# Attention state in 64-token chunks, with TensorE's slot in a new order

## The reference

```python
mod = (_silu(L0_c) @ L0_wmod).reshape(4, 6, 1, -1)     # sa, ca, ga, sb, cb, gb per sequence
h = _layernorm(x) * (1 + ca) + sa
x = x + ga * _L0_attn_ref(h, w_qkv, w_out)
h = _layernorm(x) * (1 + cb) + sb
x = x + gb * _L0_ffn_ref(h, w_router, w_gate, w_down)

# attention, per head; q, k = elu(.) + 1
def step(carry, inp):
    S, z = carry
    q_t, k_t, v_t = inp
    S = S + k_t[..., :, None] * v_t[..., None, :]
    z = z + k_t
    num = einsum('bhde,bhd->bhe', S, q_t)
    den = maximum(sum(z * q_t, -1, keepdims=True), 1e-6)
    return (S, z), num / den
```

## Time and profile before

| | us |
|---|---|
| three runs | 862.91, 864.46, 868.90 |
| median | 864.46 |
| profiled execution, span from first to last instruction | 864.3 |
| PE, PEld busy | 812.9, 667.7 |
| DVE, ACT, POOL busy | 577.1, 488.9, 478.9 |

### The profile page before, as it was taken

One profiled execution on the slowest core, in us unless ns is written; L12 is line 12 of the kernel. 1 busy time (PEld: TensorE's weight loads), 2 busy tenths in 40 slices (PEclk: granted clock), 3 DMA queues, 4 the chain that ended last, 5 costly groups with the idle time before them and its releaser, 6 DMA issues.

```text
span 864.3 us, 24637 instructions
## 1 busy us (share of the span) xinstructions
PE 812.9 (94%) x9527; PEld 667.7 (77%) x9527; DVE 577.1 (67%) x1740; ACT 488.9 (57%) x1003; POOL 478.9 (55%) x621
## 2 busy tenths in 40 slices
PE   6899999999999999999999999868999998999994
PEld 4677776777767767777777677558999998999994
DVE  5676676777777867868767767750756655767762
ACT  4665666656757656657657565442655453555551
POOL 2203345664664665646656646564556657666654
PEclk9999999999999999999999999988999999999997
DMA  5589903333332233322222212334476666676653
GB/s 195 186 247 282 284 26 114 85 87 110 67 120 89 76 114 87 86 101 70 72 71 62 64 50 41 62 85 148 82 158 120 151 145 122 152 152 158 121 100 37
DMA packets 71426, 99.02 MB, mean 115 GB/s; under 512 B 7810, under 2 KB 52866, under 8 KB 71320
## 3 DMA queue, kind: packets, MB, share of 16 engines
q1 hardware_dynamic: 38744, 53.93, 23.0%
q0 software_dynamic: 21760, 31.66, 16.2%
q10 hardware_dynamic: 10816, 11.96, 4.5%
HBM read 46.84 MB, written 63.36 MB: 127 GB/s over the span
## 4 chain that ended last, share of the span: by engine, by line
PE 75%; POOL 6%; DMA 6%; DVE 4%; issue 4%; ACT 3%; POOLq 0%; another core or an unknown queue 0%; SPq 0%; DVEq 0%; ACTq 0%
PE PJ L1436 10%; PE SCW L1662 9%; PE MD L1409 7%; PE SCW L1340 7%; PE SCW L1376 7%; PE PJ L1446 5%; PE SCW L1677 4%; PE SCW L1360 4%; PE SCW L1401 4%; DMA out<-EX,desti 3%; PE MD L1350 3%; PE SCW L1366 2%; PE SB L1677 2%; PE MD L1677 2%; POOL hT L544 2%
## 5 line engine op out<-in xcount | busy, mean ns | idle before, releaser
L494 POOL DMA_INDIRECT slot_rows<-Hrow,sloti x128 | 128.0, 1000 | 129.6 <-PE SCW L1366 48.5
L967 DVE TENSOR_TENSOR Sm<-SCW,tri 128x1024 f32<-128x1024 f32 x128 | 150.7, 1219 | 70.9 <-PE SCW L1340 69.0
L612 POOL DMA_INDIRECT out<-EX,desti x80 | 125.3, 1566 | 24.1 <-POOL idle L440 11.4
L1436 PE MATMUL PJ<-hT,w_qkv 128*128 128x512 f32 x384 | 110.1, 419 | 2.4 <-POOL hT L544 1.9
L440 POOL TENSOR_TENSOR idle<-mhalf 128x1 f32<-128x1 f32 x136 | 58.9, 433 | 78.5 <-DVE EX L1270 47.2
L1436 PEld LDWEIGHTS PJ<-hT,w_qkv 128*128 128x128 f32 x384 | 69.7, 190 | 25.1 <-issue 6.5
L1376 PE MATMUL SCW<-Sm,VA 128*17 128x128 f32 x2048 | 80.8, 275 | 0.2 <-issue 0.2
L1409 PE MATMUL MD<-w_og,ATs 128*128 128x256 f32 x256 | 73.2, 404 | 4.7 <-ACT ATs L824 2.8
L676 ACT ACTIVATE EX<-PJ 128x512 f32<-128x512 f32 x64 | 37.9, 592 | 67.5 <-PE PJ L1436 67.5
L1340 PE MATMUL SCW<-QM,KT 32*128 32x256 f32 x1024 | 73.3, 400 | 0.6 <-ACT OTs L839 0.5
L680 ACT ACTIVATE N<-X,nb,rs 128x256 f32<-128x256 f32 x128 | 66.4, 591 | 12.3 <-POOL nb L554 12.2
(11 more groups left out here) (215 smaller groups left out, 1825.4 us busy)
## 6 DMA issues: line engine op xcount, KB each, us to landing
Hrow<-slot_rows SPq DMA_DIRECT2D x32, 516.0 KB
slot_rows<-erow ACTq DMA_DIRECT2D x1, 10400.0 KB, 46.7
X<-x SPq DMA_DIRECT2D x16, 512.0 KB, 4.8
out<-X SPq DMA_DIRECT2D x16, 512.0 KB
Hrow<-mod_rows SPq DMA_DIRECT2D x16, 512.0 KB
QT<-slot_rows SPq DMA_DIRECT2D x8, 516.0 KB
slot_rows<-Hrow,sloti POOLq DMA_INDIRECT x128
N<-wd SPq DMA_DIRECT2D x4, 512.0 KB
```

Of the source, the lines that this page charges most:

```text
L494: pool.indirect_dma_start(xe, bass.IndirectOffsetOnAxis(sloti[:, par, k, t:t + 1], 0), Hrow[:, par, t, :], None, bounds_check=last_slot, o ...
L612: pool.indirect_dma_start(out, bass.IndirectOffsetOnAxis(desti[s % 2][:, a:a + 1], 0), Ys[s % 2][:, a, :], None, bounds_check=TOK - 1, oob ...
L967: dve.tensor_tensor(o.rearrange("p c (k w) -> p c k w", k=2), SCW[:, 2 * pair:2 * pair + 2, :].rearrange("p k (c w) -> p c k w", c=DC), tr ...
L1436: last = mm(PJ[m % 2][:], w_qkv[:, wp, cc, m * P:(m + 1) * P], hT[:, hp, cc, :], start=(cc + i == 0), stop=(cc == DC - 1 and i == len(SPLI ...
```

## The change

A tile's attention is cut in two chunks k of 64 tokens (`CH = P // 2`), and the state is kept for each chunk (`Sbd` with four places in turn, `state_at`). Only the two 64 x 64 blocks on the diagonal of a tile's scores are computed.

- `scores`: 16 matmuls with 32 rows x 64 weights and 128 moving columns, chunk k into partitions 64k to 64k + 63 of the same bank. SCW's four banks each use 256 of 512 columns.
- `masked_scores`: two instructions of 512 elements, each over two banks; the mask is `tri64`, a 64 x 64 triangle for either half of the partitions.
- `from_state`: per chunk 8 matmuls of 64 columns from that chunk's state; the chunk k waits for `sm_done` 2T + k + 1. `from_tile`: 32 matmuls of 64 rows x 17 weights and 64 columns, unsplit.
- `add_to_state` is done for tile n + 1 in slot n: 16 matmuls of 64 rows, fresh sums of each chunk in the new pair of banks PM, which are also PJ[1] and MD. `state` on VectorE reads them masked as `Snew` and adds twice on SBUF. At the end of a sequence the next state is set to 0. SB now takes the output product and the position sums.
- `columns_and_keys` joins the transposes of An of tile n - 1 and of the keys of tile n + 1, and ScalarE copies them by one instruction (`AK`, 512 columns).
- PE's slot: scores, (at q = 3 later) columns and keys, first stage-1 part, sums from the state, update and sums from the tile, norm transposes, product of n - 1, head rows of n, second stage-1 part. ScalarE's, VectorE's and GpSimd's orders and waits follow; the second norm is done at q = 1 in place of 2, and normalising the heads of tile n is in slot n.

The diff, cut to its core:

```diff
-        Sbd = sb("Sbd", [P, DC, 2, VW])
+        Sbd = sb("Sbd", [P, 4, DC, 2, VW])
+        Snew = sb("Snew", [P, 2, DC * 2, SW])
...
+        PM = ctx.enter_context(nc.psum_tensor("PM", [P, 2, 512], F32))
+        PJ, MD = [PJ0[:], PM[:, 0, :]], PM[:, 1, :]
...
+        OB = SCW[:, :, 0:DC * CH].rearrange("p (k b) (c i) -> p k b c i", k=2, c=DC)
...
+            def masked_scores(T):
+                dve.wait_ge(sc_full, T + 1)
+                at_least(dve, av_done, T - 1)
...
+                for b in range(2):
+                    dve.tensor_tensor(Smh(T % 2)[:, 2 * b:2 * b + 2],
+                                      SCW[:, 2 * b:2 * b + 2, 0:2 * P].rearrange("p r (m i) -> p r m i", i=CH),
+                                      tri64[:].unsqueeze(1).unsqueeze(1).to_broadcast([P, 2, 4, CH]),
+                                      ALU.mult).then_inc(sm_done, 1)
...
+            def state(n, first, second):
+                t = n + 1
+                dve.wait_ge(state_full, t + 1)
...
+                dve.tensor_tensor(Snew[:], PM[:, :, 0:DC * 2 * SW].rearrange("p k (h w) -> p k h w", h=DC * 2),
+                                  headmask[:].unsqueeze(1).to_broadcast([P, 2, DC * 2, SW]), ALU.mult
+                                  ).then_inc(state_read, 1)
+                first()
+                dve.wait_ge(state_read, t + 1)
+                dve.tensor_tensor(state_at(2 * t + 1), state_at(2 * t), Snew[:, 0], ALU.add).then_inc(sbd_half, 1)
+                second()
+                dve.wait_ge(sbd_half, t + 1)
...
+                    dve.tensor_tensor(state_at(2 * t + 2), state_at(2 * t + 1), Snew[:, 1], ALU.add).then_inc(sbd_done, 1)
...
+            def scores(T):
...
+                for cc in range(DC):
+                    for k in range(2):
+                        for r in range(4):
+                            rows = slice(32 * r, 32 * r + 32)
+                            last = mm(SCW[part(k), r, cc * P:(cc + 1) * P],
+                                      KT[rows, gp, cc, q * P + CH * k:q * P + CH * k + CH],
+                                      QM[rows, T % 2, :, cc, part(k)], start=True, stop=True, skip_group_check=True)
+                last.then_inc(sc_full, 1)
...
+            def columns_and_keys(n):
...
+                    for cc in range(DC):
+                        last = pe.transpose(MD[:, cc * P:(cc + 1) * P], a[:, cc * P:(cc + 1) * P], ident[:])
+                if tile_ok(n + 1):
+                    t = n + 1
+                    pe.wait_ge(phi_done, 4 * (t // 4) + 4)
+                    at_least(pe, ak_done, n + 1)
...
+            def from_state(T):
...
+                for k in range(2):
+                    pe.wait_ge(sm_done, 2 * T + k + 1)
+                    for cc in range(DC):
+                        for r in range(4):
...
+                            mm(OB[half, k, r // 2, cc, :],
+                               Sbd[rows, (2 * T + k) % 4, cc, :, :].rearrange("p s w -> p (s w)"),
+                               QT[rows, gp, cc, q * P + CH * k:q * P + CH * k + CH], start=(cc == 0), stop=False,
+                               skip_group_check=True)
...
+            def add_to_state(n, g, routed, step):
+                t = n + 1
...
+                    if routed and step == "columns":
+                        pe.wait_ge(h2t_done, 2 * g + 2)
...
             def logits(g, gn, stage1):
+                pe.wait_ge(state_read, min(4 * gn + 2, TILES))
                 if stage1:
                     pe.wait_ge(h_raw, 2 * (gn + 1) + 2)
...
                 if stage1 and q == 0:
-                    stage1_hi(G, 0)
-                    stage1_hi(G, 1)
-                if group_ok(gn - 1) and q == (2 if gn < GROUPS - 1 else 1):
-                    ln2_norm(it, G, gn, gp)
+                    for cidx in range(DC):
+                        stage1_transposed(G, cidx)
+                        stage1_hi(G, cidx)
+                if tile_ok(n) and tile_ok(n + 1) and q != 0:
+                    next_tile_queries(n)
+                if group_ok(gn - 1) and q == 1:
+                    ln2_norm(G, gn)
```

More of the change, by code:

```diff
@@ L28 @@
 VW = 32
+CH = P // 2
 SW = DH + 1
@@ L311, in group_ok, with head, part @@
             return 0 <= n < GROUPS
-        def halves(it, back):
-            return (it - back) // 2 if isinstance(it, int) else (it - back) // 2
-        def headslot(r):
-            return [2 * r, 2 * r + 1]
+        def head(cc, r, s):
+            return cc * HC + 2 * r + s
+        def part(k):
+            return slice(CH * k, CH * k + CH)
         @block.sync
@@ L791, in slot_ @@
                     act.activation(lgT[:], PJ[1][:, 0:P], ACT.Copy).then_inc(lgt_done, 1)
-                if tile_ok(n + 1) and q != 3:
-                    next_tile_queries(T, q, gp, tp, n)
-                if routed and step in ("first", "pick"):
-                    take(lg, lg_ps[:, :, 0:E], lg_full, g)
+                if n >= -1 and q != 3:
+                    columns_and_keys(n)
                 if routed and step == "columns":
@@ new lines, in from_tile @@
+            def from_tile(T):
+                q, gp = T % 4, (T // 4) % 2
+                if q % 2 == 0:
+                    pe.wait_ge(pj_read, 6 * (T // 4) + 5 + q // 2)
+                for cc in range(DC):
+                    for b in range(2):
+                        for k in range(2):
+                            for a in range(4):
+                                r, s = 2 * b + a // 2, a % 2
+                                last = mm(OB[32 * a:32 * a + SW, k, b, cc, :], VA[part(k), gp, q, head(cc, r, s), :],
+                                          Smh(T % 2)[part(k), r, 2 * cc + s, :], start=False, stop=True,
+                                          skip_group_check=True)
+                last.then_inc(av_done, 1)
@@ L1351, in head_rows @@
                 last.then_inc(on_full, 1)
-            def from_state(T, q, gp):
-                at_least(pe, sbd_done, T)
-                pe.wait_ge(sm_done, 2 * T + 1)
-                for cc in range(DC):
-                    for r in range(4):
-                        rows, half = slice(32 * r, 32 * r + 32), slice(64 * (r % 2), 64 * (r % 2) + 64)
-                        mm(OB[half, r // 2, cc, :], Sbd[rows, cc, :, :].rearrange("p s w -> p (s w)"),
-                           QT[rows, gp, cc, q * P:(q + 1) * P], start=(cc == 0), stop=False, skip_group_check=True)
@@ L1574, in slot_ @@
                 if tile_ok(n) and n > 0:
-                    scores(T, q, gp, tp)
-                if routed and step in ("first", "pick"):
-                    logit_rows(g)
+                    scores(n)
+                if n >= -1 and q != 3:
+                    columns_and_keys(n)
                 if n == TILES - 3:
```

449 lines of the change are left out of this document (210 added, 239 removed).

## The result

The kernel before took 865.2 us and the changed one 927.7 us on the same chip (medians of four runs each): ratio 1.073, 95% interval 1.069 to 1.077. Slower by 62 us, where 23 us less was forecast.

The account below looks back on a forecast made before the run. TensorE's instructions were taken to bound attention. Block savings of 39 us, 3 from the dropped state reload and 5 from VectorE, less 24 of added waits, made 23 us off 864.3: 841 us, range 806 to 872.

Parts of the forecast that it names:

- The step that failed: Attention's 64 tiles: TensorE is busy 518 of 535 us, so its instructions' time, block after block, sets a tile's cost.
- Rival (C): Narrow records of scores, state, tile and update supplied too slowly: break-even 14.2 ns each, 897 us at 17.5; chance 0.10.
- the block of L1391 at 285.18: State block of the kernel before, running at 14.4 ns a record behind a gap; taken as the slow bound on pace.
- PE does not wait for its rows; 0: GpSimd and SP in attention: moving row sends to other signals was priced at 0.
- wrong outright: Stated failure signs: the expert stage moves, or PE's clock falls below 1.00 in attention because of new gaps.
- Block terms: Per tile on PE: scores save 0.47 us, sums from the state cost 0.02, sums from the tile save 0.22, update costs 0.23.
- (D): Rival: only four strips run side by side though eight are addressed, in scores and sums from the tile: 875 us; chance 0.07.
- An's and the keys' transposes: On PE, joined into one block of four: 0.57 us instead of 0.37 + 0.37, saving 0.17 a tile.
- Keys behind phi: At q = 3, PE's key transposes of the next tile wait for VectorE's phi: stall 0.5 us per group, 15 groups.
- Router behind h_raw: At q = 0, PE's router matmuls wait for both of ScalarE's h_raw copies: stall 0.6 us per group, 15 groups.
- Update behind h2T: At q = 0, the state update waits until ScalarE has copied both h2T halves: stall 0.5 us per group, 15 groups.
- GpSimd is busy 287 of 535 us: Ground for pricing the moved row sends at 0; if cover failed, each held-up send costs at most 1.0 us per group.

Follow-up runs that it names:

- a_quiet: Changed kernel, gate rows loaded only for the first two groups, four of each group's 512 output rows stored: ratio 1.013 (866.8 us), second run 1.030 (889.4 us).
- a_spread: Changed kernel, output rows stored tile by tile, gate rows loaded once per batch and half: ratio 1.027 (874.8 us), second run 1.053 (907.0 us).
- a_paced: Changed kernel, SP's stores, x loads and gate rows cut to one tile's size and spread: ratio 1.023 (883.5 us), second run 1.025 (885.7 us).
- b_paced: Kernel before, with SP's transfers cut to one tile's size and spread over the tiles, as a control: 868.3 us, ratio 1.004.
- a_no_reload: Changed kernel, gate rows loaded only for the first two groups, not for each of the 16: 899.1 us, ratio to the kernel before 1.042.
- a_paced_bulk: a_paced plus, in each group of four tiles, one burst copying 512 rows of 1 KB to unread DRAM: 893.5 us, ratio 1.032.
- b_waits: Kernel before, with 120 more instructions per tile on TensorE that only check a semaphore long set: 1406.6 us, ratio 1.628.
- a_sends: Changed kernel, GpSimd's row sends at q = 1 and 2 moved off the signal that starts Snew: 924.9 us, ratio 1.071.

## Why the prediction was wrong

**Where the 61.5 us are.** Start of the output product of a tile, in us, from the PE timelines of the profiled executions:

```
                                    second runs, one chip
tile         before    after    a_quiet  a_spread  a_paced
0             40.3     44.7      44.8      44.4      45.1
20           208.1    237.3     230.0     229.5     216.8
60           546.1    600.6     562.0     578.2     558.3
63 (last)    568.8    631.5     591.5     609.0     585.9
end of span  864.3    925.8     888.2     899.0     886.0
```

The expert stage is unchanged, as forecast (295.5 before, 294.3 after). All of it lies in attention (whose last product starts at 568.8 us before, and not at 563 as the end given ahead would have it): 4.4 us before the first product, 24.8 up to tile 20, 25.3 from there to tile 60 and 8.2 behind it, less 1.2 in the expert stage. The first twenty tiles, in whose first half the loads of x and the fill of slot_rows still run, cost as much as the forty behind them; a_paced loses 3.9 us there.

**The step that failed** is the sentence from which everything is priced: "So a tile costs what TensorE's instructions for it take, one block behind the other". The records' own pace was priced, the delivery of the instructions was not. The change adds 2552 matmuls and 245 waits (+42% of the program) and shortens the time to read them; after it the sum of the blocks no longer bounds the tile. Rival (C) had "the supply of narrow records" as its heading but meant their spacing inside a block, and the blocks after run at 0.65 / 64 = 10 ns. I even had the sign in my rows: the block of L1391 at 285.18 "right behind a 0.50 us gap that no engine caused". I used it as a pace and did not ask what the engine had been without. And "PE does not wait for its rows; 0" for SP and GpSimd looked for semaphores only. No semaphore links a reload to TensorE's program.

What it cost: from the changed kernel to a_paced the ratio falls by 0.050, 43 us of the 62 (0.048 and 41 us in the second run), with TensorE's program untouched. The long gaps give 28 to 33 us of it (47.1 to 14.3 and 19.1); the rest is half clock behind them and shorter gaps. I had written that I would be "wrong outright" if the clock fell below 1.00 because of new gaps; it did, to 0.96.

**Block terms.** Right in kind, too small in sum. Scores save 0.46 a tile (forecast 0.47), sums from the state cost 0.03 (0.02), sums from the tile save 0.36 (0.22), the update costs 0.14 (0.23). Together 0.65 for 0.44: 13 us better than forecast. Eight strips do run side by side, so (D) is out. An's and the keys' transposes, forecast at 0.57 for the four, take 0.41 to 0.49 us from start to start at q = 0 to 2, so they save up to 0.33 a tile for 0.17; at q = 3 alone the keys wait for VectorE in between, as forecast under the waits.

**The three added waits.** Keys behind phi: 0.5 x 15 = 7.5 forecast, 8.2 in 15. Router behind h_raw: 9 forecast; the wait stands as "issue" at L1530, 9.9 in 11. That it is this wait shows in a_paced's second run: ScalarE's second raw copy ends at 278.35 and the router starts at 278.45. Update behind h2T: 7.5 forecast, 2.3 in 9. Sum 20.4 for 24. This part stood.

**What was missing beside the supply.** (1) Snew behind POOL's send: 14.9 us after, and 14 to 17 in the experiments on four of the five chips that ran a kernel with the sends in their new place. The prediction moved the sends to other signals and priced them at nothing, "GpSimd is busy 287 of 535 us", without asking what VectorE does at the moment at which they now start. (2) The two ends of the stage, which I never laid out: the first tile's output product comes 4.4 us later in the changed kernel, and from tile 60 to the last it is 30.9 us for 22.7. I did not test which reordering makes them. In a_paced the last stretch is 27.6 us, with one wait of 4.2 us for the last ATs. Such a wait (3.4 to 5.0 us) stands only in the paced versions of the changed kernel, and b_paced has one of 6.1 us near the same place, so it looks like a price of the pacing and not of the change.

**What is left of the forecast.** From tile 20 to tile 60, away from both ends, a tile takes (546.1 - 208.1) / 40 = 8.45 us before and 9.08 after; 8.30 in a_quiet and 8.54 in a_paced (8.32 in its first run). I had forecast 8.45 - 23 / 64 = 8.09. So with little supply trouble left the changed kernel's tile is about as long as before. In a_paced's 40 tiles (second run) TensorE is busy for 299.5 us where it was busy for 330.8 (0.78 less a tile) and idle in named waits and gaps for 42.0 where it was 5.3 (0.92 more a tile): 16.1 us go to the three forecast waits, 12.6 to Snew, and 12.6 have no releaser. The first a_quiet, on the chip without the waits for Snew, had (546.0 - 223.4) / 40 = 8.07, but that chip also ran the kernel before 1.2% quicker (854.2 for 864.7 us), so this is no proof of my figure; that the two agree is partly luck. What a version with no wait for Snew, no long gap and both ends in order would take was not shown by any run.

## What to carry to other kernels

When a change replaces few large instructions by many small ones, divide the time of a slot by its instructions and compare with the instruction queue in the DMA view: here one 16 KB packet per 9.7 us was free and one per 5.5 us was not. Then look for bulk transfers of any queue, even of data that nobody waits for: cut them to one tile's size and spread them. And when a wait is removed and nothing comes of it, look whether "issue" has grown by the same amount; then the shortage is upstream, and it has to go first.

## What the runs showed of the hardware

An instruction packet is hardly slowed by a bulk transfer but held back: it takes about 1 us once it moves (median 0.98 us after, 1.03 before), and at 320 to 327 us none moved until all but twelve of the reload's packets had started. When it was asked for, the trace doesn't show; that it was waiting is concluded from a_no_reload, where this tile's gap is 1.8 us for 4.3, and from a_paced_bulk, where bursts that no engine uses bring gaps back. The Trainium skill (DMA: Bandwidth & Descriptors, section "Queues, rings and completion order") says that an engine takes turns between queues only after a whole packet of some 9 to 17 descriptors. An estimate from that page of the Trainium skill: 512 rows on 16 engines are 32 descriptors each, two to four such turns, so a share of the burst's 7 us and hardly all of it. By the same estimate a tile's 128 rows, 8 on each engine, are gone in one turn; a_spread and a_paced agree in direction (19 long gaps to 15, and to 8 and 11).

Instructions of TensorE that only look at a semaphore long passed followed each other every 106 ns (b_waits), as much as ten of the narrow records; net of what was hidden, and with the clock's loss, the run grew by 71 ns for each.

VectorE's Snew, which reads PSUM and one operand from SBUF, started 1.4 us late when GpSimd's indirect send had started with it, and 0.3 us late in the first a_quiet and a_spread, beside the same send and 0.7 us before its end. The Trainium skill (SBUF — State Buffer, section "SBUF: two separate sides") describes a port pair that VectorE and GpSimd hold exclusively for a whole instruction, on VectorE's side when it runs in a two-port mode or reads two inputs from SBUF. Snew reads one, so that page of the Trainium skill doesn't cover it. That the delay went with the send (a_sends) fits a hold of some kind. Why it outlasts the send by 0.4 us on four chips stays open. That one chip let Snew through beside the send and the others didn't, with the same kernel, no run here explains. For a measurement it means that two kernels of this family compare only on one chip: a_spread's ratio to the kernel before was 1.027 on one and 1.053 on another, far outside both intervals.
